# Attention values as the stationary operand in column tiles, with the units of a group taken in halves

## The chip, the cores and the metric

One core of one Trainium2 chip runs the kernel. The metric is the device time of one execution in microseconds. The engines are TensorE (PE, its weight loads apart as PEld), VectorE (DVE), ScalarE (ACT), GpSimd (POOL) and SyncE (SP), which issues the DMAs.

## What is computed

The reference is two transformer-like layers on x of shape (8, 512, 128). Layer 0 (a WKV recurrence and a quantised product) isn't touched by the change. Layer 1 is an attention in three branches, mixed by a gate for each batch, and a gated cell. Its attention, cut to what matters:

```
q  = [nq @ w_dq_nope, rope(nq @ w_dq_rope)]           # 16 heads, 32 + 64 wide
k1 = [ckv @ w_dk_nope, k_rope],  v1 = ckv @ w_dv       # latent keys and values
ks, vs = projections of the 32 selected tokens
kw, vw = window keys and values, x @ w_wink, x @ w_winv
a1 = attn(q, k1, v1, causal=True)
a2 = attn(q, ks, vs, causal=False)
a3 = attn(q, kw, vw, causal=True)
out = (g0 * a1 + g1 * a2 + g2 * a3) @ w_proj
```

Each attn is softmax(q k^T * scale) v with heads of 32 values. There are 512 tokens, so 4 tiles of 128 queries, and tile t of a causal attention looks at t + 1 tiles of keys.

## The kernel before, in words

After layer 0 the attention stage runs over 8 batches with 4 groups of 4 heads each. A group has 32 **units** (`units`, L50): the causal attention a (0 is latent, 1 is window), the head h, and the query tile t in the order of `TILES`, 3, 1, 0, 2. Group 0 of batch 0 is the turn `FIRST`, then a hardware loop runs seven turns of four groups (`FULL`), then `LAST` has three groups. The order of the work is written out by hand: every engine runs its own `attend` over the steps s, and does at step s what is due for units s, s - 2, s - 3 and s - 5. A semaphore is counted up by each stage of a unit.

A unit goes through these stages:

- TensorE multiplies query tile and keys into one of three PSUM banks (L1582, K = 96, fp32, recorded as two passes), and adds the mask by a bf16 matmul (L1584).
- VectorE takes the row maximum, negated (L1306). ScalarE takes the exponential out of PSUM, with the row sum (L876).
- TensorE, two steps later (`T_LAG`), turns the t + 1 blocks of probabilities by fp32 transposes (L1609) into bank 3 or 4.
- ScalarE copies them as fp16, the high part (L856). VectorE, one step later, subtracts to get the low part in fp16 (L1311).
- TensorE, five steps after the score (`V_LAG`), multiplies: the probabilities are stationary (128 x 128, fp16), the values moving (128 x 96 in bf16, since each value is split in three bf16 parts), once for the high part (L1599) and once for the low part (L1600) of each block.

A **row** is the four units of one head and one attention. After a row VectorE adds the three parts (L1274), multiplies by gate and inverse row sum (L1284) and adds the two attentions (L1291); after a group it adds the selected attention (L1295). GpSimd makes the three bf16 parts of the values (`split_values`, L640 on).

Between them TensorE fills a shared bank, 7, by a table of steps (`group_tasks`): the projections of the next group ("x1q" to "vl"), the turned selected probabilities ("p2T") and their product ("o2"), the turned output of the group ("ocT") and its projection ("op"), and some things once a batch, among them "kr" (L1498, L1499, two strips of 64 columns) and "vs" (L1517, four strips of 32 columns). ScalarE reads the bank, or VectorE where `READER` says so. A filling waits until the one before it was read.

The value matmuls, as they stand in a step of TensorE (L1597 to L1601):

```
out = bank[5 + r % 2][:, t * 3 * VH:(t + 1) * 3 * VH]
for c in range(t + 1):
    parts = V[a][par][:, c * HG + h].rearrange("p n v -> p (n v)")
    MM(out, PTh[:, k % 4, c * P:(c + 1) * P], parts, start=(c == 0), stop=False)
    last = MM(out, PTl[:, k % 4, c * P:(c + 1) * P], parts, start=False, stop=(c == t))
```

## Time and profile before

| | |
|---|---|
| median of 3 runs | 2240.78 us (2236.99 to 2243.73) |
| profiled execution, its own time | 2239.67 us |
| its span | 2237.9 us |
| TensorE busy | 1905.6 us, 85% |
| VectorE busy | 1669.0 us, 75% |
| ScalarE busy | 1382.1 us, 62% |
| GpSimd busy | 879.9 us, 39% |
| instructions | 48381 |

Busy time is the union of the records of an engine over the span. A matmul's record runs from its start to its modelled end, and since matmuls are pipelined, the next one starts long before that; the rate is read from the starts. Layer 0 takes the first 330 us or so, and the attention stage most of the rest.

### The profile page before, as it was taken

What the parts mean: (1) busy time and instruction counts of PE and PEld (TensorE: products, weight loads), DVE (VectorE), ACT (ScalarE), POOL (GpSimd) and SP (SyncE); (2) the same over time, 40 slices, a digit from 0 to 9 for tenths busy, and PEclk for the clock granted to TensorE, in tenths of its full rate; (3) what the DMA queues carried; (4) which work ended last, traced back from release to release, by engine and by line L of the source; (5) the groups of instructions that cost most, each with busy time, mean ns of one, the idle gap of its engine ahead of it and who ended that gap; (6) DMA issues with size and microseconds to landing.
All of it is one profiled execution on the core that took longest, in us unless ns stands there. A gap on an engine that the chain in (4) does not pass through costs nothing.

```text
span 2237.9 us, 48381 instructions
## 1 busy us (share of the span) xinstructions
PE 1905.6 (85%) x13756; PEld 1306.6 (58%) x13756; DVE 1669.0 (75%) x4134; ACT 1382.1 (62%) x4244; POOL 879.9 (39%) x851
## 2 busy tenths in 40 slices
PE   4334346899989998999999999999999999999996
PEld 2212223667666766676666666666666666666762
DVE  5999952777777777677868776877687768887882
ACT  1112212677767776777767776777677767676771
POOL 0232324444434443454445434543554245434500
PEclk7655665999999999999999999999999999999997
DMA  4000001111111111111111211121112111211101
GB/s 138 0 0 0 0 2 45 44 37 45 35 44 35 40 41 45 34 36 45 44 35 35 47 44 35 35 47 44 35 35 47 44 34 35 47 44 33 36 2 38
DMA packets 71388, 81.76 MB, mean 37 GB/s; under 512 B 29521, under 2 KB 37842, under 8 KB 70994
## 3 DMA queue, kind: packets, MB, share of 16 engines
q1 hardware_dynamic: 71122, 78.55, 13.6%
q8 instruction: 126, 2.06, 0.4%
q14 instruction: 140, 1.15, 0.2%
HBM read 7.70 MB, written 2.10 MB: 4 GB/s over the span
## 4 chain that ended last, share of the span: by engine, by line
PE 70%; DVE 17%; issue 7%; ACT 3%; POOL 1%; SPq 1%; DVEq 0%; DMA 0%; ACTq 0%; POOLq 0%
PE bank L1582 23%; PE bank L1609 12%; PE bank L1483 4%; PE bank L1599 4%; PE bank L1600 4%; PE bank L1484 3%; PE bank L1584 2%; DVE arena L1311 2%; PE bank L1434 2%; PE bank L1541 2%; PE bank L1525 2%; DVE arena L1306 1%; PE bank L1479 1%; DVE arena L1074 1%; PE bank L1548 1%
## 5 line engine op out<-in xcount | busy, mean ns | idle before, releaser
L1582 PE MATMUL bank<-arena 96*128 96x512 f32 (+6 forms) x2048 | 779.1, 462 | 32.2 <-issue 22.3
L1306 DVE TENSOR_REDUCE arena<-bank 128x1 f32<-128x512 f32 (+3 forms) x1024 | 498.4, 487 | 375.0 <-PE bank L1584 365.8
L856 ACT ACTIVATE arena<-bank 128x512 f16<-128x512 f32 (+3 forms) x1024 | 449.3, 439 | 335.8 <-PE bank L1609 321.8
L876 ACT ACTIVATE arena<-bank,arena 128x512 f32<-128x512 f32 (+3 forms) x1024 | 541.8, 529 | 116.0 <-DVE arena L1306 103.9
L1609 PE MATMUL bank<-W,arena 128*128 128x128 f32 x2560 | 475.8, 284 | 46.8 <-ACT arena L876 24.6
L1311 DVE TENSOR_TENSOR arena<-bank,arena 128x512 f16<-128x512 f32 (+3 forms) x1024 | 493.1, 482 | 4.1 <-ACT arena L856 3.5
L1582 PEld LDWEIGHTS bank<-arena 96*128 96x128 f32 x2048 | 332.3, 196 | 150.8 <-issue 137.2
L1599 PEld LDWEIGHTS bank<-arena 128*128 128x128 f16 x2560 | 239.5, 98 | 179.3 <-issue 118.4
L1600 PE MATMUL bank<-arena 128*128 128x96 bf16 x2560 | 338.4, 205 | 0.0
L1599 PE MATMUL bank<-arena 128*128 128x96 bf16 x2560 | 337.5, 205 | 0.9 <-DVE arena L1311 0.9
L1609 PEld LDWEIGHTS bank<-W,arena 128*128 128x128 f32 x2560 | 279.6, 143 | 77.5 <-issue 38.5
L600 POOL TENSOR_TENSOR arena<-arena,W 128x512 f32<-128x512 f32 x64 | 69.8, 1091 | 548.6 <-ACT arena L790 548.6
L1600 PEld LDWEIGHTS bank<-arena 128*128 128x128 f16 x2560 | 228.6, 97 | 0.1
L1584 PE MATMUL bank<-maskB,identB 128*128 128x128 bf16 x1024 | 228.3, 223 | 0.0
L876 ACT ACTIVATION_READ_ACCUMULATOR arena<-bank,arena 128x1 f32 x1024 | 209.6, 205 | 0.0
L646 POOL TENSOR_TENSOR arena<-arena,one 128x512 bf16<-128x512 f32 x64 | 66.6, 1040 | 323.6 <-ACT arena L799 320.0
L1434 PE MATMUL bank<-W,arena 128*128 128x128 f32 x416 | 74.5, 308 | 122.2 <-ACT arena L748 53.2
L1584 PEld LDWEIGHTS bank<-maskB,identB 128*128 128x128 bf16 x1024 | 100.7, 98 | 113.6 <-issue 85.4
L1274 DVE TENSOR_REDUCE arena<-bank 128x128 f32<-128x384 f32 x256 | 135.1, 528 | 0.0
L1434 PEld LDWEIGHTS bank<-W,arena 128*128 128x128 f32 x416 | 52.7, 157 | 140.8 <-ACT arena L748 54.8
L1284 DVE SCALAR_TENSOR_TENSOR arena<-arena,gtc,small 128x128 f32<-128x128 f32 x256 | 118.1, 461 | 8.3 <-PE bank L1434 7.8
L1483 PE MATMUL bank<-arena,LW 96*128 96x512 f32 x192 | 116.0, 689 | 3.1 <-ACT arena L790 2.5
(265 smaller groups left out, 2833.2 us busy)
## 6 DMA issues: line engine op xcount, KB each, us to landing
arena<-arena SPq DMA_DIRECT2D x896, 64.0 KB, 2.0
arena<-arena SPq DMA_DIRECT2D x64, 128.0 KB, 2.2
W<-wide SPq DMA_DIRECT2D x1, 3538.0 KB, 12.9
X<-x SPq DMA_DIRECT2D x8, 256.0 KB, 5.6
out<-arena SPq DMA_DIRECT2D x8, 256.0 KB, 2.2
arena<-arena SPq DMA_DIRECT2D x96, 16.0 KB, 1.9
LW<-lat SPq DMA_DIRECT2D x1, 768.5 KB, 13.9
arena<-mods SPq DMA_DIRECT2D x1, 768.0 KB, 4.5
```

The source lines that it names most:

```text
L856: A(PTh[:, k % 4, 0:n], bank[3 + k % 2][:, 0:n], ACT.Copy).then_inc(s_hi, 1)
L876: A(Pb[:, s % 4, 0:n], bank[s % 3][:, lo:lo + n], ACT.Exp, bias=nmax[:, s:s + 1], accum_out=lsum[:, c:c + 1]).then_inc(s_p, 1)
L1274: v.tensor_reduce(red, parts, AX_X, ALU.add).then_inc(s_red, 1)
L1306: v.tensor_reduce(nmax[:, s:s + 1], bank[s % 3][:, lo:lo + n], AX_X, ALU.max, negate=True).then_inc(s_max, 1)
L1311: TT(PTl[:, k % 4, 0:n], bank[3 + k % 2][:, 0:n], PTh[:, k % 4, 0:n], ALU.subtract).then_inc(s_lo, 1)
L1434: last = pe.transpose(dst[:, j * P:(j + 1) * P], src[:, j], ident)
L1483: return MM(dst[:], LW[0:QL, col:col + P], latT[0:QL], start=True, stop=True)
L1582: MM(bank[s % 3][:, 0:lo + n], query(t), Kb[a][0:QD, g % 2, h, skip:skip + lo + n], start=True, stop=False)
L1584: MM(bank[s % 3][:, lo + t * P:lo + n], identB[:], maskB[:], start=False, stop=True).then_inc(s_qk, 1)
L1599: MM(out, PTh[:, k % 4, c * P:(c + 1) * P], parts, start=(c == 0), stop=False)
L1600: last = MM(out, PTl[:, k % 4, c * P:(c + 1) * P], parts, start=False, stop=(c == t))
L1609: last = pe.transpose(bank[3 + k % 2][:, c * P:(c + 1) * P], Pb[:, k % 4, c * P:(c + 1) * P], ident)
```

## The change

The units of a group now come in halves. `HALVES` puts the tall tiles (t = 3, 2) of all four heads first, then the low ones (t = 1, 0). A row is now one attention of a group, with all four heads and all tiles: 16 units, two rows a group.

The turned probabilities are kept in fp32 for a whole half (`PT`, tall and low), blocks of two tiles side by side, and moved out of PSUM once: the tall units by VectorE (three steps after the score), the low ones by ScalarE (two steps after it). The split into high and low parts is gone, and so are the three bf16 parts of the values with GpSimd's work for them; `V` is fp32.

The values are now stationary and the probabilities move. For one block c of keys, four matmuls follow each other, one a head: 128 x 32 stationary values, 256 or 128 moving columns, with the outputs in four strips of 32 partitions of bank 5. The outputs come out turned, so "ocT" is gone; "p2T" is turned in the new order of tiles, and "o2" is one matmul of 512 columns that VectorE adds to `ocT` straight from the bank.

The inverse row sums now have to lie along the columns. VectorE takes 16 inverses a row and multiplies them by the gate (step 16 of the row), GpSimd repeats each 32 times (`repeat`), TensorE turns that into bank 6 (`spread`, four transposes, step 19), ScalarE moves it (step 21), and VectorE multiplies bank 5 by it (step 23) and adds the two rows (step 24).

The diff, cut to its core:

```diff
-TILES = (3, 1, 0, 2)
+HALVES = ((3, 2), (1, 0))
...
-T_LAG, L_LAG, V_LAG = 2, 3, 5
+GR = 2
+RU = GU // GR
+T_LAG, D_LAG = 2, 3
+PV_TALL, PV_LOW = 11, 19
+INVERT, SPREAD, MOVE, NORM, ADD = 16, 19, 21, 23, 24
+MOVER = {3: "dve", 2: "dve", 1: "act", 0: "act"}
...
-READER = {"op": "dve", "ks": "dve"}
+READER = {"op": "dve", "ks": "dve", "o2": "dve"}
...
@@ GpSimd
+            def repeat(turn, r):
+
+                q, a = divmod(r, GR)
+                pool.wait_ge(s_inv, turn.r0 + (r + 1))
...
+                row = inv[:, r % 2].rearrange("p (n o) -> p n o", o=1).to_broadcast([P, NT * HG, VH])
+                pool.tensor_tensor(ivX.rearrange("p (n v) -> p n v", v=VH), row, ones_hv, ALU.mult).then_inc(s_ix, 1)
@@ ScalarE, attend
-                        A(PTh[:, k % 4, 0:n], bank[3 + k % 2][:, 0:n], ACT.Copy).then_inc(s_hi, 1)
+                        positive(s_pv, turn.half_free(k))
+                        A(turned(turn, k), turned_bank(turn, k), ACT.Copy).then_inc(s_pa, 1)
...
+                    r, late = divmod(s - MOVE, RU)
+                    if 0 <= r < n_units // RU and late == 0:
+                        act.wait_ge(s_sp, turn.r0 + (r + 1))
+                        positive(s_nrm, turn.r0 + r)
+                        A(ivT, bank[6][:], ACT.Copy).then_inc(s_iv, 1)
@@ VectorE, attend
-                        TT(PTl[:, k % 4, 0:n], bank[3 + k % 2][:, 0:n], PTh[:, k % 4, 0:n], ALU.subtract).then_inc(s_lo, 1)
+                    k = s - D_LAG
+                    if 0 <= k < n_units and MOVER[turn.units[k][3]] == "dve":
+                        v.wait_ge(s_pT, u0 + (k + 1))
...
+                        CP(turned(turn, k), turned_bank(turn, k)).then_inc(s_pd, 1)
@@ TensorE, attend
+                def values(r, low, c):
...
+                    top = 1 if low else 3
+                    n = P if c == top else 2 * P
+                    for h in range(HG):
+                        rows = slice(h * VH, (h + 1) * VH)
+                        last = MM(bank[5][rows, low * 2 * P:low * 2 * P + n], V[a][turn.g(q) % 2][:, c, rows],
+                                  PT[low][:, h, c * 2 * P:c * 2 * P + n], start=(c == 0), stop=(c == top))
+                    if c == top:
+                        last.then_inc(s_pv, 1)
+
+                def spread(r):
+                    pe.wait_ge(s_ix, turn.r0 + (r + 1))
...
+                    for n in range(NT):
+                        last = pe.transpose(bank[6][:, n * P:(n + 1) * P], ivX[:, n * P:(n + 1) * P], ident)
+                    last.then_inc(s_sp, 1)
...
-                        for c in range(t + 1):
-                            parts = V[a][par][:, c * HG + h].rearrange("p n v -> p (n v)")
-                            MM(out, PTh[:, k % 4, c * P:(c + 1) * P], parts, start=(c == 0), stop=False)
-                            last = MM(out, PTl[:, k % 4, c * P:(c + 1) * P], parts, start=False, stop=(c == t))
-                        last.then_inc(s_pv, 1)
+                    for low, at, parts in ((0, PV_TALL, 4), (1, PV_LOW, 2)):
+                        r, c = divmod(s - at, RU)
+                        if 0 <= r < n_units // RU and c < parts:
+                            values(r, low, c)
```

TensorE's order inside the loop. Before, most of one step of a group: every step has score and mask, two to eight value matmuls of one unit, and the transposes of another (L numbers are those of the kernel before):

```order
L1582 MATMUL bank2<-arena 128x288 [waits probs_ready]
L1584 MATMUL bank2<-maskB,identB 128x128
L1591 REGISTER_ALU
L1599 MATMUL bank6<-arena 128x96 [waits probsT_low_ready,row_read]
L1600 MATMUL bank6<-arena 128x96
L1599 MATMUL bank6<-arena 128x96
L1600 MATMUL bank6<-arena 128x96
L1599 MATMUL bank6<-arena 128x96
L1600 MATMUL bank6<-arena 128x96
L1599 MATMUL bank6<-arena 128x96
L1600 MATMUL bank6<-arena 128x96
L1605 REGISTER_ALU
```

Now, one step and the beginning of the next, with tall scores, where the low half of the row before is multiplied (L1639 is the score, L1641 the mask, L1601 `values`, L1612 `spread`, L1660 the transposes):

```order
L1639 MATMUL bank1<-arena 128x384 [waits probs_ready]
L1641 MATMUL bank1<-maskB,identB 128x128
L1601 MATMUL bank5<-arena 32x256 [waits probsT_moved_by_act,probsT_moved_by_dve]
L1601 MATMUL bank5<-arena 32x256 x3
L1607 REGISTER_ALU
L1612 MATMUL bank6<-W,arena 128x128 [waits row_inverses_moved,row_inverses_repeated]
L1612 MATMUL bank6<-W,arena 128x128 x3
L1652 REGISTER_ALU
L1660 MATMUL bank4<-W,arena 128x128 [waits probsT_moved_by_act,probs_ready]
L1660 MATMUL bank4<-W,arena 128x128 x2
L1639 MATMUL bank2<-arena 128x512 [waits probs_ready]
L1641 MATMUL bank2<-maskB,identB 128x128
```

The value matmuls no longer stand in every step: they stand in six of 16, four heads at a time, between a mask of full width and transposes of full width, and the waits on the low part have become waits on the moves.

VectorE's order at the start of a loop turn. Before, one row maximum and one subtraction a unit:

```order
L1306 TENSOR_REDUCE arena<-bank0 128x1 [waits scores_ready]
L1311 TENSOR_TENSOR arena<-bank3,arena 128x512 [waits probsT_high_ready]
L1306 TENSOR_REDUCE arena<-bank1 128x1 [waits scores_ready]
L1311 TENSOR_TENSOR arena<-bank4,arena 128x256 [waits probsT_high_ready]
L1306 TENSOR_REDUCE arena<-bank2 128x1 [waits scores_ready]
L1311 TENSOR_TENSOR arena<-bank3,arena 128x128 [waits probsT_high_ready]
L1306 TENSOR_REDUCE arena<-bank0 128x1 [waits scores_ready]
L1311 TENSOR_TENSOR arena<-bank4,arena 128x384 [waits probsT_high_ready]
```

Now (L1331 is the maximum, L1338 the copy of a tall tile), with no subtraction ahead of which ScalarE must have copied:

```order
L1331 TENSOR_REDUCE arena<-bank2 128x1 [waits scores_ready]
L1331 TENSOR_REDUCE arena<-bank0 128x1 [waits scores_ready]
L1338 COPY arena<-bank3 128x4x128 [waits half_pv_done,probsT_in_psum]
L1331 TENSOR_REDUCE arena<-bank1 128x1 [waits scores_ready]
L1338 COPY arena<-bank4 128x3x128 [waits half_pv_done,probsT_in_psum]
```

The copy waits for the transposes and for a free half of `PT`. In the low half VectorE has the maximum alone.

## Rows read from the trace of the kernel before

**Rows 1.** The page: span, busy time of each engine, chain of waits by engine
```profile
span 2237.9 us, 48381 instructions
...
PE 1905.6 (85%) x13756; PEld 1306.6 (58%) x13756; DVE 1669.0 (75%) x4134; ACT 1382.1 (62%) x4244; POOL 879.9 (39%) x851
...
PE 70%; DVE 17%; issue 7%; ACT 3%; POOL 1%; SPq 1%; DVEq 0%; DMA 0%; ACTq 0%; POOLq 0%
```

**Rows 2.** Windows, one batch: us, busy PE, PEld, DVE, ACT, POOL, PEclk, DMA, GB/s
```profile
1369.90:1598.60 228.70, 217.95 (x1671) 152.39 (x1671) 174.81 (x434) 165.11 (x519) 101.50 (x93) 0.98 0.16 40
```

**Rows 3.** The page, costliest groups of instructions
```profile
L1609 PE MATMUL bank<-W,arena 128*128 128x128 f32 x2560 | 475.8, 284 | 46.8 <-ACT arena L876 24.6
L1311 DVE TENSOR_TENSOR arena<-bank,arena 128x512 f16<-128x512 f32 (+3 forms) x1024 | 493.1, 482 | 4.1 <-ACT arena L856 3.5
...
L1600 PE MATMUL bank<-arena 128*128 128x96 bf16 x2560 | 338.4, 205 | 0.0
L1599 PE MATMUL bank<-arena 128*128 128x96 bf16 x2560 | 337.5, 205 | 0.9 <-DVE arena L1311 0.9
```

**Rows 4.** Groups by form: tile shapes kept apart
```profile
L1306 DVE TENSOR_REDUCE arena<-bank 128x1 f32<-128x512 f32 x256 | 176.7, 690 | 100.4 <-PE bank L1584 94.3
L1311 DVE TENSOR_TENSOR arena<-bank,arena 128x512 f16<-128x512 f32 x256 | 174.2, 680 | 0.0
...
L1306 DVE TENSOR_REDUCE arena<-bank 128x1 f32<-128x384 f32 x256 | 142.3, 556 | 119.6 <-PE bank L1584 118.5
L1311 DVE TENSOR_TENSOR arena<-bank,arena 128x384 f16<-128x384 f32 x256 | 140.6, 549 | 1.4 <-ACT arena L856 1.1
...
L646 POOL TENSOR_TENSOR arena<-arena,one 128x512 bf16<-128x512 f32 x64 | 66.6, 1040 | 323.6 <-ACT arena L799 320.0 <-POOL arena L652 3.3
...
L1295 DVE TENSOR_TENSOR arena<-arena 128x512 f32<-128x512 f32 x32 | 34.4, 1074 | 3.6
```

**Rows 5.** Waits: engine line <- releaser: us in total, times, longest
```profile
DVE arena L1306 <- PE bank L1584: 365.8, 487, 11.8
...
PE bank L1609 <- ACT arena L876: 24.6, 35, 3.4
...
PE bank L1609 <- DVE arena L1311: 21.4, 36, 2.0
```

**Rows 6.** Timeline, TensorE, value matmuls: start us, us of all merged, engine, line
```profile
1006.87 0.20 PE L1599 MATMUL bank<-arena 128*128 128x96 bf16 x1
1006.91 0.20 PE L1600 MATMUL bank<-arena 128*128 128x96 bf16 x1
...
1007.16 0.21 PE L1600 MATMUL bank<-arena 128*128 128x96 bf16 x1
```

**Rows 7.** Timeline, TensorE, around one filling "vs" (L1517)
```profile
1965.63 0.40 PE L1609 MATMUL bank<-W,arena 128*128 128x128 f32 x2
1965.96 0.43 PE L1517 MATMUL bank<-W,arena 128*32 128x128 f32 x8
1966.32 1.13 PE L1582 MATMUL bank<-arena 96*128 96x512 f32 x2
1967.28 0.22 PE L1584 MATMUL bank<-maskB,identB 128*128 128x128 bf16 x1
```

**Rows 8.** Timeline, TensorE, around one filling "kr" (L1498, L1499)
```profile
1901.87 0.64 PE L1498 MATMUL bank<-arena,W 128*64 128x512 f32 x1
...
1902.88 1.12 PE L1582 MATMUL bank<-arena 96*128 96x512 f32 x2
1903.85 0.22 PE L1584 MATMUL bank<-maskB,identB 128*128 128x128 bf16 x1
```

**Rows 9.** Timeline, TensorE, two transposes and a 512-column score, undisturbed
```profile
1359.36 0.39 PE L1609 MATMUL bank<-W,arena 128*128 128x128 f32 x2
1359.59 1.02 PE L1582 MATMUL bank<-arena 96*128 96x512 f32 x2
1360.44 0.22 PE L1584 MATMUL bank<-maskB,identB 128*128 128x128 bf16 x1
```

More of the change, by code:

```diff
@@ L82, in group_tasks @@
     if not first:
-        out += [(steps["ocT"], "ocT", q - 1), (steps["op"], "op", q - 1)]
+        out += [(steps["op"], "op", q - 1)]
     if not (last and g == NG - 1):
@@ L771, in positive @@
             def positive(sem_, value):
-                if not (isinstance(value, int) and value == 0):
+                if not (isinstance(value, int) and value <= 0):
                     act.wait_ge(sem_, value)
@@ L898, in _ @@
                 if READER.get(name, "act") == "act":
-                    read(turn, name, NG - 2 if name == "ocT" else 0)
+                    read(turn, name, 0)
             with act.Fori(0, B // 2) as i:
```

235 lines of the change are left out of this document (123 added, 112 removed).

## The prediction

> **What bounds the kernel now.** I read the page first, for who is busy and who ends the chain; then the windows of one batch, for the steady state; then the waits; and last the timeline of single matmuls, because the change replaces one form of matmul by another. The page [rows 1] shows TensorE busy 85% of the span and 70% of the chain. The windows [rows 2] show one batch of the attention stage: it takes 228.7 us, TensorE works in 218 of them at a granted clock of 0.98 (of 2.4 GHz), while VectorE has 175 and ScalarE 165. The waits [rows 5] say the same from the other side: VectorE's row maxima wait 365.8 us for TensorE, and TensorE's turning matmuls (L1609) wait only 24.6 us for exponentials and 21.4 us for VectorE's low part. So the stage goes at TensorE's rate of issue. VectorE and ScalarE lie beside it, and what they save is worth at most what TensorE still waits for them.
>
> The mean durations of matmuls [rows 3] overlap each other, so they are no price. The price is the distance from one start to the next, which only the timeline shows.
>
> **What goes.** 2560 + 2560 value matmuls [rows 3]: an fp16 stationary tile of 128 columns, 96 moving columns, one pass. Eight of them start between 1006.87 and 1007.16 [rows 6], which is 0.29 us for seven steps, 0.042 us each. 5120 x 0.042 = **-215 us**. The turn of the outputs ("ocT", four 128-column transposes in 32 groups) goes too. Two transposes take 1359.36 to 1359.59 [rows 9], 0.115 us each, so 128 x 0.115 = **-15 us**. "o2" becomes one matmul of 512 columns (two passes, 0.85 us [rows 9]) in place of four of 128 with two passes each, 8 x 0.115 = 0.92 us: 32 x 0.07 = **-2 us**.
>
> **What comes on TensorE.** Per row (16 units; two rows a group, 64 in all) there are six blocks of four matmuls. The four heads have 32 stationary columns each and write four separate partition strips of bank 5. Four blocks have 256 moving columns (256 blocks in all) and two have 128 (128 in all). The decisive question is whether four such fp32 matmuls run side by side. The kernel before has such a block already, the filling "vs" (L1517): four matmuls, 32 stationary columns each, 128 moving, fp32, each recorded as two passes. In [rows 7] the eight records start at 1965.96 and the next matmul starts at 1966.32. One after the other they would take eight passes of 0.107 us (the 0.85 us of two 512-column passes [rows 9], by columns), 0.85 us; they took 0.36. So they do run side by side.
>
> But the block costs something at both edges. Ahead of it, two transposes need 0.33 us (1965.63 to 1965.96) where two undisturbed ones need 0.23 [rows 9], so 0.10 us. Behind it, the 512-column score takes 0.96 us (1966.32 to 1967.28) where it takes 0.85 undisturbed [rows 9], so 0.11 us. The same is seen at the filling "kr" with two strips of 64 columns and 512 moving: 1.01 us inside and 0.97 us for the score behind [rows 8]. A block of 128 columns thus costs 0.10 + 0.36 + 0.11 = 0.57 us.
>
> A block of 256 columns is not in the trace. From below it is bounded by the 128-column block (0.36 us inside), from above by the 512-column one (1.01 us inside). Since both passes go by columns I interpolate: 0.36 + 128 x (1.01 - 0.36)/384 = 0.58 inside, 0.79 with its edges. Sum: 256 x 0.79 + 128 x 0.57 = 202 + 73 = **+275 us**. The edges are not paid once: a row's six blocks stand in six different steps, each between a score and a transpose of full width, so they are paid 384 times, 384 x 0.21 = 81 us.
>
> The Trainium skill (TensorEngine Tiling (Array Packing), Key Properties) says that changing the tiling mode drains TensorE; by that rule, the trace agrees, with 0.10 us at each edge. The same page (Theoretical Speedup) gives up to 4 times for 32 columns; its rule alone, without the drain, is rival A below. The Trainium skill (TensorE: Matmul & The Clock Gate, Weight-path perf modes) also says that fast weight load is on for 128 stationary columns that aren't fp32; this case shows the old matmuls at 0.042 us a pair of load and product, and no run here shows them without it.
>
> "spread" turns the repeated inverses, four transposes a row: 256 x 0.115 = **+29 us**.
>
> **Beside TensorE.** VectorE loses the subtractions of the low part (L1311, 493 us [rows 3]) and every small per-head step. It gains 512 copies of the tall tiles (0.68 and 0.55 us, priced by L1311's own forms of these sizes [rows 4]: 256 x 1.23 = 315 us), 64 norms and 32 "o2" sums of about 0.68 us, and 32 sums of two SBUF operands (1.07 us, L1295 [rows 4]). ScalarE loses the copies of the tall tiles. GpSimd loses the splitting of the values (eight operations a group, the first of them 1.04 us, L646 [rows 4]) and gains one such operation a row. I cost all of this at nothing: it lies under TensorE, as both engines had over 50 us a batch free before [rows 2] and have more now. If that cover went, rival B would be the price.
>
> **The waits.** TensorE's 46 us at L1609 [rows 5] stay in part. The half that is for exponentials is unchanged, and the half that is for the low part loses one hop (ScalarE's copy ahead of VectorE's subtraction), so I take -15 us; the ends are -46 (all gone) and +46 (as much again). The new waits are at the first block of each half, on the last move, and at "spread", on GpSimd. Behind both are the transposes of that step, and ScalarE's or VectorE's next move waits for those. The move of unit 7 is issued at step 10 and its block stands at step 11; the inverses are begun at step 16 and turned at step 19. Steps take 228.7/128 = 1.79 us [rows 2], so the three steps (5.4 us) cover one GpSimd operation of 1.04 us [rows 4] and the two short ones on VectorE. No DMA is added and SP's queue is unchanged.
>
> **The sum.** -215 - 15 - 2 + 275 + 29 - 15 = **+57 us**. Against the profiled execution of 2239.67 us that is 2297; the median of the runs, 2240.78, is 1 us above it, so the forecast is **2297 us**, 2.5% slower. A measurement of this kernel can tell about 0.3% (7 us) from no change. The likeliest case by itself reaches from 2265 to 2330: its ends come from the waits (-46 or +46 for -15, which rarely come with the other end below) and a 256-column block of 0.50 or 0.66 us inside (256 x 0.08 = 20 us either way).
>
> **Rivals.**
> A, *faster, since the edges cost nothing*. TensorE might load the next weights under the block, or the 0.10 us at each edge might be particular to the fillings, which wait for the shared bank. Then 384 x 0.21 = 81 us leave the sum: 2297 - 81 = 2216, and with all the waits gone 2185. It decides from both edges together at 0.06 us a block: 0.15 below what the rows show, and 384 x 0.15 = 57. For it: the old value matmuls follow scores with no edge at all [rows 6]. Against it: "vs" and "kr" both show the edge, and the second one is at a matmul that the fillings have nothing to do with. Chance 0.12.
> B, *slower still, since the tall half is VectorE's*. Two tall units ask VectorE for maxima of 0.69 + 0.56 and moves of 0.68 + 0.55 [rows 4], 2.48 us, where TensorE needs about 0.85 + 0.64 for the scores and 7 x 0.115 for transposes, 2.4 us with the masks, before fillings. Where no filling stands, TensorE waits for the moves; at 0.5 us a pair in half of the 256 tall pairs that is 64 us, 2361. Against it: most tall steps carry a filling of 0.85 us. Chance 0.08.
> C, *the strips don't run side by side* when moving tiles differ as they do here. Then a row streams 5120 columns at 0.85/512 = 0.00166 us, 8.5 us, in place of 1280 columns, 2.1 us: 64 x 6.4 = 410 us, about 2700. "vs" has four different moving tiles too, so chance 0.03.
> D, *no change*: the waits fall by 46 and the stretches between blocks close up, 2235 to 2260. Chance 0.07.
>
> **Numbers.** The sum holds: 0.70. Faster is A and a sliver of D: 0.13. Within 0.3%: 0.05. Slower: 0.82. The range from 2230 to 2345 takes in the forecast and D, and leaves out A, C and most of B.
>
> **What would show it.** In the profile after: the blocks (L1601) as eight records each that start within some 0.5 us, the next full-width matmul 0.58 us after the start of a 256-column block, and two transposes ahead of a block at 0.33 us; about 235 us a batch in the windows; VectorE near 1230 us busy; TensorE still the chain. Wrong would be an edge under 0.05 us (A), waits of TensorE for VectorE's copies (L1338) above 60 us (B), or a block of over 1.5 us (C).

## The result, and the profile after

The changed kernel takes 2326.75 us (median of 4 runs, 2323.01 to 2335.09). The kernel before took 2241.48 us in the same comparison. The ratio is 1.039, with a 95% interval of 1.035 to 1.042: **slower by 3.9%**, 85 us. The forecast was 2297 us in a range from 2230 to 2345. The sign and the mechanism held; 30 us of the loss weren't in the forecast.

The page after, span, busy times and chain (it answers to [rows 1]); the profiled execution took 2324.1 us:

```profile
span 2322.3 us, 41323 instructions
...
PE 1962.4 (85%) x11644; PEld 1136.9 (49%) x11644; DVE 1338.8 (58%) x2950; ACT 1142.2 (49%) x3732; POOL 644.6 (28%) x659
...
PE 74%; DVE 14%; issue 7%; ACT 2%; POOL 1%; DVEq 1%; SPq 1%; DMA 0%; ACTq 0%; POOLq 0%
```

TensorE carries 2112 matmuls fewer and is busy 57 us longer. All other engines have less to do: VectorE 330 us less, ScalarE 240, GpSimd 235. None of that shortened anything. (VectorE's 1339 us are also 109 more than the 1230 of the forecast.)

The costliest groups (they answer to [rows 3]; columns: busy, mean ns of one, idle before and its releaser):

```profile
L1331 DVE TENSOR_REDUCE arena<-bank 128x1 f32<-128x512 f32 (+3 forms) x1024 | 501.4, 490 | 701.0 <-PE bank L1641 691.4
...
L1660 PE MATMUL bank<-W,arena 128*128 128x128 f32 x2560 | 486.7, 288 | 45.7 <-DVE arena L1338 33.4
...
L1338 DVE COPY arena<-bank 128x512 f32<-128x512 f32 (+1 forms) x512 | 314.6, 614 | 0.0
...
L1601 PE MATMUL bank<-arena 128*32 128x256 f32 (+1 forms) x3072 | 225.2, 366 | 10.6 <-DVE arena L1338 7.6
```

VectorE's maxima wait 691 us for TensorE, where they waited 366 [rows 5]: VectorE is idle more and is still waited for, since the transposes (L1660) wait for its copies (L1338). The list of waits (us in total, times, longest) has that on both of TensorE's queues, matmuls and weight loads:

```profile
PEld bank L1660 <- DVE arena L1338: 106.1, 196, 2.2
...
PEld bank L1660 <- ACT arena L895: 84.1, 213, 1.0
...
PE bank L1660 <- DVE arena L1338: 33.4, 41, 1.9
```

The windows (us, busy times and counts of PE, PEld, DVE, ACT, POOL, then PEclk, DMA, GB/s) answer to [rows 2]. The first two are turns of the loop with the same work; the third is a stretch inside a turn of the first kind:

```profile
1160.60:1403.00 242.40, 226.32 (x1400) 132.27 (x1400) 132.76 (x285) 134.78 (x453) 71.45 (x68) 0.94 0.15 37
1403.00:1638.50 235.50, 220.33 (x1400) 128.15 (x1400) 132.66 (x285) 134.77 (x453) 71.47 (x68) 0.97 0.15 38
...
1268.80:1282.30 13.50, 13.50 (x71) 9.93 (x71) 3.62 (x13) 3.31 (x12) 0.00 (x0) 0.50 0.04 7
```

A turn took 228.7 us before. Now some take about 235.5, which is what the forecast said ("about 235"), and others 242.4. The difference between the two kinds stands in the column of the clock: the long turns have a stretch at a granted clock of 0.50 (1.2 GHz) that the short ones don't have, and half of its 13.65 us is 6.8 us. Five such stretches stand in the trace (three of 13.65 us, two of 17.07), each behind the same step, which comes seven times. The kernel before has none there.

They aren't the only stretches at 0.50. Both kernels have one of 10 us or more around the end of each turn, and the change has another in all seven turns of the loop, of 3.4 us, directly behind the wait of TensorE for `normed_out` (L1246, below), where the kernel before has none:

```profile
1367.70:1371.10 3.40, 3.40 (x13) 1.60 (x11) 1.41 (x3) 2.11 (x6) 0.00 (x0) 0.50 0.40 100
```

From 400 us, behind layer 0, to 80 us before the end, the stretches at 0.50 add up to 78 us in the trace of the kernel before and to 171 us in that of the change.

The timeline ahead of that stretch (start us, us of all merged, engine, line; in brackets the idle time and its releaser):

```profile
1262.23 2.33 DVE L1214 TENSOR_SCALAR arena<-W,rankT 128x32 f32<-128x32 f32 x4
...
1264.09 0.22 PE L1641 MATMUL bank<-maskB,identB 128*128 128x128 bf16 x1
...
1264.48 0.67 DVE L1221 TENSOR_TENSOR arena<-arena,bank 128x512 f32<-128x512 f32 x1
1265.28 0.29 DVE L1331 TENSOR_REDUCE arena<-bank 128x1 f32<-128x128 f32 x1
1265.48 0.68 DVE L1338 COPY arena<-bank 128x512 f32<-128x512 f32 x1
...
1266.22 0.44 PE L1660 MATMUL bank<-W,arena 128*128 128x128 f32 x2 [1.91 <-DVE arena L1338]
```

Four picks (`pick`, L1214, 2.33 us together) and the addition of "o2" (L1221, new on VectorE) stand in one step ahead of the copy of a tall tile. TensorE has issued all that it may and stops for 1.91 us. The clock falls to 0.50 some 0.6 to 2.6 us behind the end of the stop, in five of the seven turns.

The blocks themselves, TensorE's timeline (same columns), a low half:

```profile
1212.09 0.60 PE L1639 MATMUL bank<-arena 96*128 96x256 f32 x2
1212.53 0.22 PE L1641 MATMUL bank<-maskB,identB 128*128 128x128 bf16 x1
1212.68 0.64 PE L1601 MATMUL bank<-arena 128*32 128x256 f32 x8
1213.25 0.44 PE L1660 MATMUL bank<-W,arena 128*128 128x128 f32 x2
1213.52 0.38 PE L1639 MATMUL bank<-arena 96*128 96x128 f32 x2
```

Eight records, and the next matmul 0.57 us after the first of them: four strips side by side, as forecast (0.58). Ahead of the block, mask to block takes 0.15 us, where mask to transposes takes 0.06 without a block (1263.26 to 1263.32 in the same trace): an edge of 0.09 to 0.10. Behind it, two transposes take 0.27 us (1213.25 to 1213.52) where they take 0.23 undisturbed [rows 9]: an edge of 0.04 to 0.05, not 0.11.

One more reading closes the books. TensorE's timeline of a turn, cut at every start and summed by the matmul that begins each interval, so that a wait counts to the matmul ahead of it (us a turn; act_all is an experiment below):

| interval begins with | before | after, short turn | after, long turn | act_all |
|---|---|---|---|---|
| score | 76.6 | 77.8 | 79.1 | 78.3 |
| mask | 8.1 | 21.3 | 21.7 | 12.0 |
| value matmul | 40.6 | 29.4 | 30.6 | 27.1 |
| of these, the last one up to the next turn | 4.4 | 5.8 | 5.9 | 3.5 |
| transposes | 43.0 | 46.0 | 46.5 | 45.8 |
| "spread" | | 4.1 | 4.1 | 4.1 |
| fillings | 60.6 | 57.1 | 59.9 | 57.7 |
| turn | 228.9 | 235.7 | 241.8 | 225.0 |

The 640 old value matmuls of a turn would take 26.9 us at 0.042. They have 40.6: 4.4 is the end of the turn, and 9.3 is time in which the transposes waited, by the list for the low part and for exponentials. That is 75 us in eight batches, more than the 46 of [rows 5], because a wait is listed only from the end of the record ahead of it, and such a record lasts 0.20 us. The kernel before, in between value matmuls and transposes, with nothing in brackets:

```profile
1211.49 0.21 PE L1599 MATMUL bank<-arena 128*128 128x96 bf16 x1
1211.53 0.21 PE L1600 MATMUL bank<-arena 128*128 128x96 bf16 x1
1211.73 0.52 PE L1609 MATMUL bank<-W,arena 128*128 128x128 f32 x3
```

0.20 us from the last value matmul to the transposes, of which 0.16 is a wait. After, the waits stand behind the masks. In act_all, where they are gone, the masks have 12.0 us: 128 of 0.06 and 48 edges of 0.09. The change has 21.3, so 9.3 us of waits a turn, the same as the kernel before had.

### The profile page after: what moved, and what is told of

Same layout as the page of the kernel before. It is cut to its first block, busy times and chain, and to the rows that moved or that the text cites. A ratio compares the mean times of both kernels' runs of the same rounds, so it can differ in the third digit from the quotient of the medians.

```text
span 2322.3 us, 41323 instructions
## 1 busy us (share of the span) xinstructions
PE 1962.4 (85%) x11644; PEld 1136.9 (49%) x11644; DVE 1338.8 (58%) x2950; ACT 1142.2 (49%) x3732; POOL 644.6 (28%) x659
## 4 chain that ended last, share of the span: by engine, by line
PE 74%; DVE 14%; issue 7%; ACT 2%; POOL 1%; DVEq 1%; SPq 1%; DMA 0%; ACTq 0%; POOLq 0%
PE bank L1639 24%; PE bank L1660 13%; PE bank L1601 9%; PE bank L1511 4%; PE bank L1512 3%; DVE arena L1338 2%; PE bank L1641 2%; PE bank L1612 2%; PE bank L1553 2%; PE bank L1534 2%; PE bank L1507 1%; PE bank L1549 1%; PE bank L1566 1%; DVE arena L1098 1%; PE bank L1574 1%
## 5 line engine op out<-in xcount | busy, mean ns | idle before, releaser
L1331 DVE TENSOR_REDUCE arena<-bank 128x1 f32<-128x512 f32 (+3 forms) x1024 | 501.4, 490 | 701.0 <-PE bank L1641 691.4
L1639 PE MATMUL bank<-arena 96*128 96x512 f32 (+6 forms) x2048 | 794.2, 470 | 43.9 <-issue 34.4
L1660 PE MATMUL bank<-W,arena 128*128 128x128 f32 x2560 | 486.7, 288 | 45.7 <-DVE arena L1338 33.4
L1660 PEld LDWEIGHTS bank<-W,arena 128*128 128x128 f32 x2560 | 284.4, 143 | 326.8 <-issue 125.3
L1639 PEld LDWEIGHTS bank<-arena 96*128 96x128 f32 x2048 | 342.2, 199 | 187.6 <-issue 155.2
L1338 DVE COPY arena<-bank 128x512 f32<-128x512 f32 (+1 forms) x512 | 314.6, 614 | 0.0
L674 POOL TENSOR_TENSOR arena<-arena,one 128x512 f32<-128x512 f32 x64 | 66.7, 1042 | 886.9 <-DVE arena L1305 877.0
L875 ACT ACTIVATE arena<-bank 128x256 f32<-128x256 f32 (+1 forms) x512 | 168.9, 330 | 285.3 <-PE bank L1660 284.4
L1601 PE MATMUL bank<-arena 128*32 128x256 f32 (+1 forms) x3072 | 225.2, 366 | 10.6 <-DVE arena L1338 7.6
L1641 PE MATMUL bank<-maskB,identB 128*128 128x128 bf16 x1024 | 230.7, 225 | 0.0
L1641 PEld LDWEIGHTS bank<-maskB,identB 128*128 128x128 bf16 x1024 | 101.8, 99 | 118.3 <-issue 91.0
L1462 PE MATMUL bank<-W,arena 128*128 128x128 f32 x160 | 36.6, 371 | 123.2 <-ACT arena L775 52.9
L891 ACT ACTIVATE arena<-bank 128x32 f32<-128x32 f32 (+1 forms) x384 | 78.8, 205 | 94.2 <-DVE arena L1331 87.1
L1601 PEld LDWEIGHTS bank<-arena 128*32 128x32 f32 x3072 | 61.6, 109 | 126.3 <-issue 103.9
L1512 PE MATMUL bank<-arena,W 128*128 128x512 f32 x192 | 102.3, 615 | 4.3 <-ACT arena L817 3.6
L634 POOL TENSOR_TENSOR arena<-arena 128x512 f32<-128x512 f32 x64 | 81.2, 1268 | 41.7 <-DMA arena<-arena 34.0
L817 ACT ACTIVATE arena<-bank 128x512 f32<-128x512 f32 x128 | 76.2, 595 | 32.4 <-PE bank L1511 16.5
## 6 DMA issues: line engine op xcount, KB each, us to landing
LW<-lat SPq DMA_DIRECT2D x1, 768.5 KB, 13.9
```

Source lines behind the costliest of these rows:

```text
L634: step(pool.tensor_tensor(stX1, rt[:, 2], rt[:, 3], ALU.subtract))
L875: A(turned(turn, k), turned_bank(turn, k), ACT.Copy).then_inc(s_pa, 1)
L891: made = A(p2h[:, h, tiles], scores, ACT.Copy)
L1331: v.tensor_reduce(nmax[:, s:s + 1], bank[s % 3][:, lo:lo + n], AX_X, ALU.max, negate=True).then_inc(s_max, 1)
L1338: CP(turned(turn, k), turned_bank(turn, k)).then_inc(s_pd, 1)
L1512: return MM(dst[:], w("wink", col, P), hTc, start=True, stop=True)
```

## The experiments

The theory at this point: the blocks cost what the timeline says, and the rest of the loss is TensorE waiting for VectorE's copy, with a lower clock behind the longest of these waits. The rivals: the edges of the blocks are dearer than they look; the strips don't really overlap; or it is the order of the units (tall side by side) and not the copies. Ratios are against the kernel before, which measured between 2240.4 and 2241.2 us beside them.

### picks_early: the longest wait taken apart

```diff
-                        tokens(turn.nb, at - 20)
-                    if g == 2 and at == 24:
+                        made = tokens(turn.nb, at - 20)
+                        if at == 20 + NT - 1:
+                            made.then_inc(s_zc, 1)
+                    if g == 2 and at == 12:
+                        v.wait_ge(s_c, turn.nb)
...
-                            last = pick(turn.nb, j)
-                        last.then_inc(s_zc, 1)
+                            step(pick(turn.nb, j))
```

> The changed kernel with VectorE's four picks for the selected tokens (2.33 us in one piece) moved from step 24 of group 2, where they stand right ahead of the o2 sum that the change gave to VectorE, to step 12. Theory 1 (the stall of 2.13 us before the transposes at that place, once a loop turn, and the 13.65 us at 1.2 GHz that follow it in five of seven turns, are this pile-up): the stall goes, the 13.65 us at the lower clock go with it, the slow turns of 242.4 us come down to about 234, and the time falls by 35 to 50 us, to about 2285. Theory 2 (the lower clock comes from TensorE's work being thinner over the whole turn, wherever it waits): only the stall itself goes, 8 times 2 us or less, 2310 to 2320, and the stretches at the lower clock stay or move.

As the first theory expected: 2288.25 us, ratio 1.0205 [1.0188, 1.0223], 38.5 us less than the change. TensorE's waits for the copies fall less than that:

```profile
PE bank L1662 <- DVE arena L1338: 25.6, 41, 0.8
```

As many waits as before, 7.8 us less in total, the longest 0.8 in place of 1.9. So most of the 38.5 us didn't lie in the waits. The turns show where:

```profile
1375.50:1610.80 235.30, 222.54 (x1400) 129.54 (x1400) 133.03 (x285) 135.20 (x453) 71.46 (x68) 0.96 0.15 38
```

The turns between the ends of the loop take 234 to 238 us, none 242, and the mean granted clock rises from 0.892 to 0.903. The stretches of 13 and 17 us at the old place of the picks are gone, and the sum of all falls from 171 to 123 us. Four small instructions in an unlucky step cost 1.7% of the kernel.

### blocks_paired: half of the edges

```diff
-                        if 0 <= r < n_units // RU and c < parts:
-                            values(r, low, c)
+                        if 0 <= r < n_units // RU and 2 * c < parts:
+                            values(r, low, 2 * c)
+                            values(r, low, 2 * c + 1)
```

> The changed kernel with two value blocks in one step (tall blocks 0 and 1, then 2 and 3, low 0 and 1), so that a row goes into the 32-column form three times and not six: 192 entries and exits fewer. If each entry and exit costs what the profile of the changed kernel shows (0.10 us ahead, about 0.04 us behind, and 0.03 us of exposed first weights inside), the time falls by 192 x 0.17 = 33 us, to about 2294. If the edges were free or lay where TensorE waits anyway, nothing moves. If a block must wait for the one before it (both add into the same bank), it gets slower by up to 192 x 0.2 = 38 us.

2298.93 us, ratio 1.0258 [1.0241, 1.0275], 27.8 us less than the change. 192 pairs of edges are gone, so a pair of them is worth 27.8/192 = 0.145 us. The timeline says 0.10 + 0.04 = 0.14. The edges are real, and nearer to that size than to my 0.21. That the two agree so closely is partly luck: this run's trace has 184 us at 0.50 where the change's has 171, and without these 14 us more the gain would have been some 6 us larger (an estimate, by the price of the lower clock worked out below), 0.18 a pair.

### tall_act: the same copies, exchanged

```diff
-MOVER = {3: "dve", 2: "dve", 1: "act", 0: "act"}
+MOVER = {3: "act", 2: "act", 1: "dve", 0: "dve"}
```

> The changed kernel with the movers exchanged: the tall tiles of the turned probabilities are moved by ScalarE, two steps after the score, and the low ones by VectorE. If TensorE's waits for VectorE's copies in the tall half and just behind it (33.4 us at the transposes by the profile, and the 2.13 us stalls behind the picks) are a matter of VectorE's load there, they fall: 2285 to 2300. If they are a matter of the length of the way from score to exponential to transpose, they stay or become waits for ScalarE, which also has the exponentials: 2320 to 2340.

2244.35 us (10 runs), ratio 1.0014 [1.0004, 1.0024], 82 us less than the change, with not one instruction of TensorE different. Its waits:

```profile
PE bank L1660 <- DVE arena L1338: 7.0, 11, 0.7
```

One line brings back nearly all of the loss, more than either theory expected. Summed as above, the masks have 13.9 us a turn in place of 21.3. Two things differ in it: which engine copies the tall tiles, and that ScalarE's copies are issued two steps after the score and VectorE's three. move_step2 below separates them.

### before_picks2: a longer stall put into the kernel before

```diff
                         for j in range(NT):
+                            TS(gi[:, P + j * KEEP:P + (j + 1) * KEEP], w("iota"), rankT[:, j, ds(turn.nb, 1)], None,
+                               ALU.is_equal)
                             last = pick(turn.nb, j)
```

> The kernel before with the four picks of step 24 of group 2 done twice (the second time into a part of a tile that nobody reads then): 2.3 us more of VectorE in one piece at the place where the changed kernel stalls. Theory 1 (a stall of about 2 us of TensorE there is followed by a stretch at 1.2 GHz): TensorE gets a stall of 1 to 3 us there, the granted clock falls behind it for 3 to 14 us in most turns, and the time rises by 20 to 60 us. Theory 2: it rises by at most 8 x 2.3 = 18 us and the clock stays as it was.

2266.27 us, ratio 1.0113 [1.0096, 1.0130]: four extra small instructions of VectorE a turn, on an engine that isn't the bottleneck, cost 25.5 us, 3.6 us a turn. TensorE stops at that place, and in three of the turns a stretch at 1.2 GHz stands behind the stop:

```profile
1235.07 0.63 PE L1611 MATMUL bank<-W,arena 128*128 128x128 f32 x4 [1.97 <-DVE arena L1311]
```

```profile
1235.70:1252.50 16.80, 16.80 (x80) 14.04 (x80) 7.46 (x23) 5.57 (x17) 0.00 (x0) 0.50 0.03 5
```

So the mechanism isn't particular to the changed kernel. But a stop of this length isn't enough by itself: here it stands in all seven turns, and four have no stretch behind it. The unchanged kernel has stops of 1.5 to 2.0 us in five turns of its own trace, one with a stretch of 3.4 us behind it and four with none:

```profile
1250.17 0.52 PE L1609 MATMUL bank<-W,arena 128*128 128x128 f32 x3 [1.84 <-DVE arena L1311]
```

### act_paired_picks: the three together

```diff
-MOVER = {3: "dve", 2: "dve", 1: "act", 0: "act"}
+MOVER = {3: "act", 2: "act", 1: "dve", 0: "dve"}
...
-                        if 0 <= r < n_units // RU and c < parts:
-                            values(r, low, c)
+                        if 0 <= r < n_units // RU and 2 * c < parts:
+                            values(r, low, 2 * c)
+                            values(r, low, 2 * c + 1)
...
-                    if g == 2 and at == 24:
+                    if g == 2 and at == 12:
...
```

> The changed kernel with the three edits that gained alone, together: movers exchanged (tall tiles by ScalarE), two value blocks in a step, the picks at step 12. Alone they gave -82, -28 and -38 us. Theory 1 (the first and the third take away the same stalls and the same stretches at 1.2 GHz, the second takes away time in which TensorE is busy): the first and third overlap nearly wholly and the second adds: 2205 to 2225, faster than both kernels. If they were independent, it would be 2179. If the second only filled waits that the first removed, it would stay at 2240.

2254.09 us, ratio 1.0056 [1.0038, 1.0074]. A miss: 10 us slower than tall_act alone. (The picks' part of the diff is that of picks_early.) The gains don't add up. What the waits show is that the copies of the low tiles, now VectorE's, are late behind the pairs:

```profile
PE bank L1663 <- DVE arena L1338: 26.7, 63, 1.5
```

### one_strip: the strips one after the other

```diff
-                        last = MM(bank[5][rows, low * 2 * P:low * 2 * P + n], V[a][turn.g(q) % 2][:, c, rows],
-                                  PT[low][:, h, c * 2 * P:c * 2 * P + n], start=(c == 0), stop=(c == top))
+                        last = MM(bank[5][0:VH, low * 2 * P:low * 2 * P + n], V[a][turn.g(q) % 2][:, c, rows],
+                                  PT[low][:, h, c * 2 * P:c * 2 * P + n], start=True, stop=True)
```

> The changed kernel with all four heads' value matmuls written to one strip (partitions 0 to 31 of bank 5), each started and stopped by itself, so that no two of them can run side by side; the values' sums over key blocks are left out, and heads 1 to 3 are overwritten or missing. Work, forms and places stay. If the four strips ran side by side (the blocks of 0.57 and 0.36 us), a row now streams 5120 columns in place of 1280, 64 x 6.4 = 410 us more, about 2730. If they only ran in pairs, about 130 us more. If they never ran side by side, nothing changes.

This kernel leaves out the sums over the key blocks, and the heads overwrite each other in the one strip.

2692.36 us in one run, 366 us more than the change. TensorE's timeline, a block of 128 columns, here and in the change:

```profile
1202.97 1.06 PE L1601 MATMUL bank<-arena 128*32 128x128 f32 x8
1203.97 0.66 PE L1660 MATMUL bank<-W,arena 128*128 128x128 f32 x4
```

```profile
1200.84 0.43 PE L1601 MATMUL bank<-arena 128*32 128x128 f32 x8
1201.19 0.66 PE L1660 MATMUL bank<-W,arena 128*128 128x128 f32 x4
```

1.00 us in place of 0.35. A block of 256 columns takes 1.85 us from start to start where nothing waits, in place of 0.57. By these, the kernel should lose 128 x 0.65 + 256 x 1.28 = 411 us; it lost 366, at a mean granted clock of 0.922 in place of 0.892. The strips run side by side in the change; rival C had the price right (410) for a case that didn't occur.

### spread_one: one of the four transposes of "spread"

```diff
-                    for n in range(NT):
-                        last = pe.transpose(bank[6][:, n * P:(n + 1) * P], ivX[:, n * P:(n + 1) * P], ident)
+                    last = pe.transpose(bank[6][:, 0:P], ivX[:, 0:P], ident)
```

> The changed kernel with one of the four transposes that turn the repeated inverses; three quarters of the inverses are left out. By the forecast's price 192 x 0.115 = 22 us less, about 2305, and a little more if the clock gains by it. If those transposes lay in time in which TensorE waits, nothing moves.

This kernel leaves out three quarters of the inverses.

2300.45 us, ratio 1.0266 [1.0249, 1.0284], 26.3 us less than the change. 192 transposes are gone, which would be 0.137 us each against the 0.115 of the sum. That isn't their price alone: this trace has a stretch at 0.50 behind the picks in seven turns where the change has it in five, and TensorE's stop at the end of a turn is 4.1 to 4.5 us in place of 5.3 to 6.2. From start to start, "spread" takes 1.4 us a turn in place of 4.1, and 2.7/24 = 0.11 us for each, as forecast.

### before_tiles: only the order, in the kernel before

```diff
-TILES = (3, 1, 0, 2)
+TILES = (3, 2, 1, 0)
```

> The kernel before with the tiles of a head in the order 3, 2, 1, 0: two tall units follow each other and then two low ones, which is a small piece of what the halves do. If putting tall units side by side costs by itself (VectorE and ScalarE are late behind them, TensorE waits), it gets slower by 10 to 40 us, 2250 to 2280. If the order is harmless and the surplus lay in what the change gave to VectorE, it stays within 7 us of 2241.

2285.12 us, ratio 1.0199 [1.0179, 1.0219]: the kernel before loses 44.7 us when tall and low tiles aren't mixed. The work is the same to the instruction. TensorE's waits for the low part more than double, from 21.4 us [rows 5], and the turn of the outputs now waits too (8.6 us before):

```profile
PE bank L1609 <- DVE arena L1311: 49.3, 74, 1.3
...
PE bank L1434 <- DVE arena L1265: 31.7, 24, 1.4
```

`TILES` mixed tall units with short ones so that VectorE caught up after each. The halves of the change give that up, and my sum had no term for it. The two rows rise by 51 us, the second of them at a step that the change doesn't have, and the stretches at 0.50 rise from 78 to 133 us in this run. How much of the 44.7 us the change pays for its order isn't shown.

### act_all: VectorE moves nothing

```diff
-MOVER = {3: "dve", 2: "dve", 1: "act", 0: "act"}
+MOVER = {3: "act", 2: "act", 1: "act", 0: "act"}
...
-                        pe.wait_ge(s_pd, turn.moved(last_unit, "dve"))
-                        pe.wait_ge(s_pa, turn.moved(last_unit, "act"))
+                        for who, moved in (("dve", s_pd), ("act", s_pa)):
+                            if who in MOVER.values():
+                                pe.wait_ge(moved, turn.moved(last_unit, who))
```

> The changed kernel with all turned probabilities moved by ScalarE, two steps after the score, none by VectorE. The exchange of the movers gave -82 us though it moved the low tiles to VectorE, three steps after. Theory 1 (what costs is that VectorE, which has the maxima and the bunched small work, also moves): no engine gets near TensorE's load (ScalarE about 1310 us busy), TensorE's last waits for VectorE's copies go too, and the time is 2215 to 2240. Rival (ScalarE, which has the exponentials, becomes late in the tall half): TensorE waits for ScalarE, 2250 or more.

2200.72 us, ratio 0.9824 [0.9807, 0.9840]: 126 us less than the change and **40 us less than the kernel before**. Between its ends, the loop's turns take 225.0 to 225.7 us, at 0.98:

```profile
1106.90:1332.20 225.30, 215.44 (x1400) 127.69 (x1400) 98.72 (x221) 158.99 (x517) 71.48 (x68) 0.98 0.16 40
```

ScalarE is busy 159 us of a turn and VectorE 99; the work sits on the busier of the two and is done in time there. That nothing of 2 us stands in ScalarE's queue may be why; no run tested it. TensorE's matmuls wait for a copy once (0.4 us), its weight loads for 55.4 us. The stretches at 0.50 add up to 65 us, less than in the kernel before: about 50 of the 126 us (an estimate, by the price below) are the clock.

### act_paired: exchanged movers and pairs

The first two parts of the diff of act_paired_picks.

> Movers exchanged and two value blocks in a step, the picks left at step 24. The three edits together gave 2254 us where the exchange alone gave 2244. If the picks at step 12 were what spoilt it (they are 2.3 us of VectorE in the low half, where VectorE now moves the low tiles), this is about 2217, the exchange less the 28 us of the pairing. If the pairing spoils it (a longer block puts the transposes behind it, and VectorE's low copies, late, and TensorE is granted the lower clock more often), it stays at 2245 to 2260.

2242.25 us (10 runs), ratio 1.0005 [0.9995, 1.0015]: pairs gain 27.8 us in the change and 2 us here. Against act_paired_picks only the place of the picks differs: with these movers step 12 costs 12 us, where it gained 38.5 with the movers of the change. The intervals of a turn show that the gain was made and given back. Value matmuls and "spread" together take 30.4 to 31.2 us a turn where tall_act has 34.2 to 34.6, about 3.6 less, as 24 pairs of edges of 0.145 say. But the masks, which have 24 edges fewer, take 2.1 us more, the scores 1.1 and the fillings 0.6: TensorE arrives earlier and waits for VectorE's copies of the low tiles instead.

```profile
PE bank L1661 <- DVE arena L1338: 21.3, 56, 1.5
```

tall_act had 7.0 there.

### act_all_best: the version that beats both

act_all with the pairs of blocks_paired, the picks of picks_early, and the turn of `normed_out` one step later:

```diff
-        extra = [] if first else [(17, "z4T"), (20, "gf"), (21, "gi"), (24, "gc")]
+        extra = [] if first else [(18, "z4T"), (20, "gf"), (21, "gi"), (24, "gc")]
```

> All moves by ScalarE, two value blocks in a step, the picks at step 12 (where VectorE then moves nothing), and the filling z4T one step later, at 18, so that VectorE's normalisation for it (2.06 us of step 16) is done. Each takes away a wait or busy time of its own: against the movers on ScalarE alone 28 us for the pairing and 8 x 1 to 2 us for z4T, so 2170 to 2205, 2 to 3% faster than the kernel before. If, as with the exchange, the pairing brings back the waits and the lower clock, 2215 to 2240.

2186.90 us, ratio 0.9764 [0.9747, 0.9780]: 2.4% faster than the kernel before, 140 us faster than the change. The three additions bring 13.8 us on top of act_all. Two turns, from the first score of one to that of the next:

```profile
1098.00:1321.20 223.20, 211.92 (x1401) 130.78 (x1401) 99.52 (x221) 157.68 (x517) 71.95 (x68) 0.97 0.16 40
1321.20:1545.30 224.10, 212.83 (x1401) 131.30 (x1401) 99.46 (x221) 157.88 (x517) 71.99 (x68) 0.97 0.16 40
```

act_all takes 225.0 to 225.7 there: 1 to 3 us a turn, in each turn. No run tells the three additions apart.

### move_step2: the same movers, one step earlier

```diff
-T_LAG, D_LAG = 2, 3
+T_LAG, D_LAG = 2, 2
```

> The changed kernel with VectorE moving the tall tiles as the change has it, but two steps after the score, not three, so that its copy of unit s - 2 stands behind the maximum of unit s and not behind that of unit s + 1. It tells apart why ScalarE as the only mover gained 126 us. Theory 1 (the place: the transposes of step s wait for the move of unit s - 4, which VectorE began only after the maximum of unit s - 1, in the very step before; a step earlier it is done in time): 2200 to 2225, and TensorE's waits for VectorE's copies (33.4 us at the transposes, 106 us at their weights) shrink to under 10 and 40 us. Theory 2 (the load: VectorE with maxima, moves, selected part and picks is too full in the tall half): 2290 or more, and the waits stay.

2250.04 us (6 runs, 2243.36 to 2266.88), ratio 1.0041 [1.0017, 1.0066], 77 us less than the change. VectorE moves the same tiles with the same instructions; they only stand one step earlier in its queue. What is left of TensorE's waits for these copies, on both of its queues:

```profile
PEld bank L1601 <- DVE arena L1338: 21.2, 26, 1.5
PE bank L1601 <- DVE arena L1338: 14.6, 22, 1.3
PEld bank L1660 <- DVE arena L1338: 3.2, 14, 0.2
```

The 106.1 us of the loads at L1660 have become 3.2, and in the sums of a turn the masks fall from 21.3 to 14.6 us. The waits at the value blocks (L1601) have grown, from 7.6 to 14.6 us, and the time is above the 2200 to 2225 that the theory of the place expected. Of the 126 us that act_all gains, 77 are to be had by the place of the copy.

Most of them aren't had by the clock. The profiled run is the slowest of the six, with the mean granted clock of the change's (0.892), and takes 2266.88 us against 2324.10: 57 us at the same clock. Its stretches at 0.50 add up to 174 us, as in the change (171). The stretch behind the picks stands in all seven turns, and the stop ahead of it has become shorter:

```profile
1237.51 0.64 PE L1601 MATMUL bank<-arena 128*32 128x256 f32 x8 [1.28 <-DVE arena L1338]
```

```profile
1239.50:1253.10 13.60, 13.60 (x72) 9.72 (x70) 3.68 (x13) 3.81 (x14) 0.00 (x0) 0.50 0.05 7
```

## Why the prediction was right, and where it wasn't

**What bounds the kernel.** "So the stage goes at TensorE's rate of issue" held: VectorE, ScalarE and GpSimd lost 805 us of busy time between them and the kernel became slower. That what they save is worth nothing was right. That what they still do is hidden was not.

**Side by side.** Right, and tested both ways: 0.57 us inside for 256 columns (0.58 forecast), 0.35 for 128, and 1.00 for 128 when all four strips are one (one_strip). Rival C is out.

**The edges.** The step "Behind it ... 0.11 us" failed in size. I had taken it from a 512-column score behind "vs"; here transposes follow, and it is 0.04. With 0.10 + 0.57 + 0.04 = 0.71 us for 256 columns and 0.10 + 0.36 + 0.04 = 0.50 for 128, the blocks cost 256 x 0.71 + 128 x 0.50 = 246 us, not 275. blocks_paired gives 0.145 (0.18 if its lower clock is allowed for) a block for both edges, against rival A, which needed 0.06. The Trainium skill (TensorEngine Tiling (Array Packing), Key Properties) says that a change of the tiling mode drains TensorE; the runs agree, with 0.145 us for the way in and out.

**"spread".** 4.1 us a turn from start to start, 33 us in all, where the forecast had 29.

**The waits.** "I take -15 us" is the step that failed. I had counted hops of data (one fewer) and not looked at the queue in which the copy stands. VectorE copies a tall tile three steps after its score, behind the maximum of that step and whatever else stands there, and the transposes of the next step wait for it. The waits did not fall: 9.3 us a turn before, 9.3 after. The ends were wrong as well. "All gone" I had put at -46 from the list of waits; by start-to-start intervals it is 8 x 9.3 = 75 us, and act_all gained them. The runs put numbers on the mechanism: 77 us for one step (move_step2; 57 at the same clock), 38.5 for the picks with the clock behind them (picks_early), 82 for exchanged engines (tall_act). They overlap and aren't to be added.

Rival B named the mechanism, with tall units that ask VectorE for more than a step has, and priced it at 64 us. It had a chance of 0.08 because "most tall steps carry a filling". What happened is the forecast with a good part of rival B. Its sign, waits for VectorE's copies above 60 us, came out on one queue only: TensorE's matmuls list 41 us (L1660 and L1601), its weight loads 127.5.

**The fixed steps of VectorE.** "I cost all of this at nothing" failed at two places. The addition of "o2" joins the picks ahead of a tall copy (1.91 us of stop), and the four instructions that make `normed_out` (L1246, 2.06 us) now stand directly ahead of TensorE's turn of it, which waits 2.2 us in each turn of the loop, where it waited 0.5 before:

```profile
1366.82 0.63 PE L1462 MATMUL bank<-W,arena 128*128 128x128 f32 x4 [2.22 <-DVE arena L1246]
```

The 1.7 us more are most of the 3.0 that the transposes gained in the table, where a wait counts to the matmul ahead of it. The end of the turn costs 1.4 us more (4.4 to 5.8).

**The clock.** It had no term. A long turn takes 6.1 us more than a short one (241.8 - 235.7), with the same work and 13.0 us more at 0.50: 0.47 us lost for each. At this price the 92 us more at 0.50 in the change (171 - 78, before rounding) are about 43 us, half of the loss. That is an estimate; at the ends of the turns, where TensorE stops anyway, the lower clock costs less.

**The account.** A short turn costs 6.8 us more than before: value matmuls less waits and less the end of the turn 23.6 - 26.9 = -3.3 (that is, 29.4 - 5.8 against 40.6 - 9.3 - 4.4), edges at the masks 12.0 - 8.1 = +3.9, waits 9.3 - 9.3 = 0, transposes +3.0, "spread" +4.1, fillings -3.5 (the turn of the outputs is among them), scores +1.2, end of the turn +1.4. Eight batches x 6.8 = 54 us, and five low stretches x 6.1 = 31 us: 85 us, and 85 were measured.

That it closes so well is partly luck. Cut from first score to first score, the seven turns of the loop take 1679.7 us in place of 1597.3, 82 more; what lies ahead of them takes 2 more and what lies behind them the same. The turn of the table is the longest of the steady ones before (227.9 to 228.9); against the turns at the same places the two short ones lose 7.8 and 7.7 us. And the 6.8 hold some clock as well: the 3.4 us at 0.50 in each turn follow directly behind the wait for `normed_out` and cost about 1.6 us a turn at the price above.

The forecast's 57 came close to the first part by errors of opposite sign: blocks 29 too dear, against waits, fixed steps and the end of the turn too cheap. The clock it lacked. So the range was met with part of its sum wrong, and its own ends don't follow from its terms: waits at +46 in place of -15 are 61 us, 2358, above the 2330 of the likeliest case and the 2345 of the range.

**Left open.** What brings on a low stretch. The length of the stop ahead of it doesn't decide: at the picks 1.91 us is followed by one five times in seven in the change and seven times in spread_one, 1.28 us seven times in move_step2, 1.97 us three times in before_picks2, and in act_all the stop of 2.2 us ahead of the turn of `normed_out` by none, where the change has 3.4 us at 0.50 behind it each time. What makes the end of a turn 1.4 us longer is open too; act_all has it 2.3 us shorter, but spread_one has it about 1.3 us shorter with VectorE's copies as they are, so these alone don't explain it.

## What to carry to other kernels

Price a tiled block of matmuls from start to start with both edges, and take each edge beside the neighbour that it will really have. When work moves to an engine with room to spare, look at the queue in front of each moved instruction: an engine that is 58% busy held up the one that sets the time, because its copies stood late in the queue, and one step earlier was worth 77 us. Add up the time at the lower clock in both traces before explaining a difference: here it carried about half of the loss, and it moved in nearly every experiment. Take waits from start to start, not from the list alone. Try the placement (who copies, at which step) before judging the idea; here the change at 3.9% slower and a version 2.4% faster than the kernel before differ in little else.

## What the runs showed of the hardware

A stop of TensorE of 1 to 2 us can be followed by a cost several times its length: behind the one at the picks (1.91 us) the granted clock stood at 0.50 for 13.65 us, with TensorE busy in all of it, and the turn was 6.1 us longer by the table. In before_picks2 the stretch shown was 16.8 us behind a stop of 1.97 us, and in move_step2 13.6 us behind one of 1.28 us. Stops of 1.5 to 2.2 us had nothing behind them in the kernel before (four of five) and, at the wait for `normed_out`, in act_all (seven of seven).

The edge behind a block isn't fixed: 0.11 us ahead of a score of 512 columns [rows 7, 9], 0.04 to 0.05 us ahead of transposes. Four fp32 matmuls in strips of 32 columns take 0.57 us for 256 moving columns, and 1.85 us when all four write the same strip (one_strip).

A list of waits can miss a third of them. TensorE's short value matmuls start every 0.042 us and have records of 0.20 us, so the first 0.16 us of a wait behind one is inside a record; 46 us listed were 75 us from start to start (the 75 as what was left over by the sums of one turn, times eight).
